# Pairing the key and the query phase chains in the attention stage of a layer kernel on eight cores

## The reference

```python
xn = layernorm(x)
key, value, query = xn @ Wk + bk, xn @ Wv + bv, xn @ Wq + bq
key_phase   = tanh(key @ Wkp + bkp) * phase_scale
query_phase = tanh(query @ Wqp + bqp) * phase_scale
mem_real = cumsum over chunks of 64 tokens of (value * cos(key_phase))
mem_imag = cumsum over chunks of 64 tokens of (value * sin(key_phase))
retrieved = (mem_real * cos(query_phase) + mem_imag * sin(query_phase)) / sqrt(D)
attn = xn + (layernorm(retrieved) * ln_g + ln_b) @ Wo + bo
h = concat([xn, -xn]); w(k) = where(k, 1, -1)
ffn = s2 * (2*relu(s1 * (2*relu(s0 * (h @ w(k0))) @ w(k1))) @ w(k2))
return x + attn + ffn
```

## Time and profile before

| | us |
|---|---|
| median of 3 runs | 2515.23 |
| lowest, highest of them | 2512.86, 2683.95 |
| the profiled execution | 2516.47 |
| its span, from the first to the last instruction of the slowest core (core 5) | 2514.9 |
| spans of the eight cores | 2495.7 to 2514.9 |
| TensorE busy | 1976.2 (79% of the span) |
| VectorE busy | 440.0 (17%) |
| ScalarE busy | 390.3 (16%) |
| GpSimd busy | 89.8 (4%) |

### The profile page before, as it was taken

One profiled execution on the slowest core, in us unless ns is written; L12 is line 12 of the kernel. 1 busy time (PEld: TensorE's weight loads), 2 busy tenths in 40 slices (PEclk: granted clock), 3 DMA queues, 4 the chain that ended last, 5 costly groups with the idle time before them and its releaser, 6 DMA issues.

```text
span 2514.9 us, 21260 instructions; the slowest of 8 cores (2495.7 to 2514.9 us)
## 1 busy us (share of the span) xinstructions
PE 1976.2 (79%) x8836; PEld 868.4 (35%) x8836; DVE 440.0 (17%) x518; ACT 390.3 (16%) x439; POOL 89.8 (4%) x40
## 2 busy tenths in 40 slices
PE   4525435665647769999969999996999996999997
PEld 1213111221224434444424444442344442444443
DVE  0043665555544420000000000000000000000000
ACT  1220333444420002000002000002100001200000
POOL 0001441000000000000000000000000000000000
PEclk9755767777767779999989999998999998999998
DMA  6701569999012346554434645235654343644542
GB/s 102 181 21 35 156 166 168 178 215 186 1 34 96 102 137 170 149 149 135 119 101 135 181 134 146 81 108 176 174 151 136 101 134 117 178 140 136 149 115 69
DMA packets 227081, 324.47 MB, mean 129 GB/s; under 512 B 4645, under 2 KB 103077, under 8 KB 226986
## 3 DMA queue, kind: packets, MB, share of 16 engines
q1 hardware_dynamic: 181930, 235.02, 33.2%
q0 software_dynamic: 32576, 71.31, 16.1%
q10 hardware_dynamic: 12480, 16.78, 1.8%
HBM read 281.16 MB, written 67.11 MB: 138 GB/s over the span
## 4 chain that ended last, share of the span: by engine, by line
PE 73%; DVE 10%; DMA 6%; issue 5%; ACT 5%; DVEq 0%; POOL 0%; ACTq 0%; SPq 0%; POOLq 0%
PE ps L762 36%; PE ps L743 9%; PE ps L790 9%; PE ps L497 4%; PE ps L666 3%; PE ps L352 2%; DMA kst<-k0dbf 2%; DVE wA L519 2%; DVE ph L516 2%; PE ps L714 1%; PE ps L769 1%; PE ps L443 1%; DMA stK<-wkT 1%; PE ps L772 1%; DVE ph L513 1%
## 5 line engine op out<-in xcount | busy, mean ns | idle before, releaser
L762 PE MATMUL ps<-h_sb,kst 128*128 128x512 bf16 x4096 | 901.9, 381 | 10.8 <-DVE rows_sb L725 5.5
L762 PEld LDWEIGHTS ps<-h_sb,kst 128*128 128x128 bf16 x4096 | 397.2, 98 | 511.4 <-issue 47.1
L743 PE MATMUL ps<-xn_sb,kst 128*128 128x512 bf16 x1024 | 230.2, 389 | 84.0 <-DMA kst<-k0dbf 84.0
L719 DVE COPY rowsf_sb<-ps 1x512 f32<-1x512 f32 x8 | 5.4, 678 | 1325.5 <-PE ps L714 1325.5
L790 PE MATMUL ps<-h_sb,kst 128*128 128x512 bf16 x1024 | 223.7, 379 | 6.5 <-DVE rowsf_sb L723 2.2
L776 ACT ACTIVATE h_sb<-ps,cols_sb 128x1024 bf16<-128x1024 f32 x64 | 71.3, 1114 | 932.7 <-PE ps L772 932.7
L534 PE MATMUL ps<-brb,u_sb 128*128 128x512 bf16 x32 | 16.6, 518 | 219.4 <-DVE brb L567 189.8
L743 PEld LDWEIGHTS ps<-xn_sb,kst 128*128 128x128 bf16 x1024 | 101.9, 100 | 212.0 <-issue 97.1
L790 PEld LDWEIGHTS ps<-h_sb,kst 128*128 128x128 bf16 x1024 | 99.0, 98 | 130.5 <-issue 13.5
L748 ACT ACTIVATE h_sb<-ps,cols_sb 128x1024 bf16<-128x1024 f32 x64 | 71.3, 1114 | 415.4 <-PE ps L743 415.4
L666 PE MATMUL ps<-xh_fm,wo_sb 128*128 128x256 bf16 x512 | 84.4, 321 | 29.0 <-DVE x L688 27.5
(11 more groups left out here) (122 smaller groups left out, 1127.3 us busy)
## 6 DMA issues: line engine op xcount, KB each, us to landing
k1bf<-k1t POOLq DMA_DIRECT2D x2, 16384.0 KB, 97.6
kst<-k0dbf SPq DMA_DIRECT2D x64, 512.0 KB, 4.1
xtm_sb<-x_tm SPq DMA_DIRECT2D x16, 512.0 KB, 13.2
st_a<-k0t POOLq DMA_DIRECT2D x8, 1024.0 KB, 8.4
st_b<-k0b POOLq DMA_DIRECT2D x8, 1024.0 KB, 10.2
k0dbf<-st_dd SPq DMA_DIRECT2D x8, 1024.0 KB, 6.8
k2bf<-k2t POOLq DMA_DIRECT2D x1, 8192.0 KB, 116.0
x<-x_fm SPq DMA_DIRECT2D x8, 1024.0 KB, 5.4
```

The source lines that it names most:

```text
L743: e.matmul(ps[:, nco * TF:(nco + 1) * TF], lhsT=kb[:, kc * 256 + nco * 128:kc * 256 + nco * 128 + 128], rhs=xn_v[:, kc, t0:t0 + TF], start ...
L762: e.matmul(ps[:, nco * TF:(nco + 1) * TF], lhsT=kb[:, kc * 256 + nco * 128:kc * 256 + nco * 128 + 128], rhs=h1[:, kc * TF:(kc + 1) * TF], ...
```

## The change

The two calls of `trig_ops` of a group are made one behind the other at the loop's start, and their instructions are emitted in pairs: the key's tanh, the query's tanh, the key's product, the query's product, and so on. The query's chain therefore stands ahead of `bib`, `brb`, the first cumulative sums and the two projections, instead of behind them. Nothing else is changed: the same instructions on the same buffers.

```diff
     a1_A(0)
     for gg in range(NG):
-        a1_emit(trig_ops(PS[1], 0))
+        kp_ops = trig_ops(PS[1], 0)
+        qp_ops = trig_ops(PS[2], 1)
+        for i in range(len(kp_ops)):
+            a1_emit([kp_ops[i], qp_ops[i]])
         P.emit("dve", lambda e: e.tensor_tensor(bib[:], PS[0][:], wA_[0][:], op=ALU.mult),
                reads=[PS[0], wA_[0]], writes=[bib])
...
             tmproj_xn("v", "bv", gg + 1, PS[0])
             tmproj_xn("k", "bkp", gg + 1, PS[1])
-        a1_emit(trig_ops(PS[2], 1))
         a1_combine(gg, 0)
```

## The result

The changed kernel takes 2558.30 us (median of 10 runs) against 2516.29 us (10 runs): 42 us more, a ratio of 1.0166 with a 95% interval of 1.0155 to 1.0177. The forecast was 2546 us, 30 us more, in a range of 2526 to 2570. The sign, the class (slower, but by less than 2%) and the range held; the size came out 12 us short.

A forecast was written before the change was run, and what follows sets the result against it. Bound by the key's ScalarE-VectorE chain, then TensorE's projections, in each gap between attention groups; 5.1 - 5.6 + 38.2 - 8.0 = +29.7 us on 2516.47 gives 2546 us, range 2526 to 2570.

The forecast's parts named there:

- The late gaps: Eleven later gaps between attention groups: each uncovered part grows by 3.47 us, projections' part unchanged; +38.2 us.
- The last group: Final attention group, with no projections following: combine of half 0 starts right behind the sums; -8.0 us.
- The first group: Start of attention: query tanh waits for its projection, first sums at 266.57 instead of 261.46; +5.1 us.
- this subtraction is past: GpSimd's subtraction at 263.63, in the first group: taken as over for the hits, which were counted from 266.6 on.
- The early gaps: First four gaps between groups: 143.3 instead of 148.84 us, three of seven subtractions holding VectorE on the path; -5.6 us.
- the price of a held pair: VectorE instructions held by a GpSimd subtraction in the early gaps: 6.7 us for each of three hits.
- the next falls beside the projections: Early gaps: if one subtraction meets the trigonometric part, the following one comes where blocked VectorE has over 8 us to spare.
- Nothing for the later stages: Stages after attention: they keep their order and shift as a whole, 0 us.
- the subtractions leave the path: Rival, early gaps: GpSimd's subtractions no longer hold the bounding path; 20 us less, 2526 us; chance 0.10.
- all seven stay on it: Rival, early gaps: all seven subtractions hit the bounding path; 27 us on top, 2573 us; chance 0.10.
- TensorE's clock: Rivals, projections after each pause: full clock, 2514 us, chance 0.02; wholly at 1.2 GHz, 2620 us, chance 0.01.
- The rule of the shared port pair: VectorE with two SBUF inputs or in two-port mode and GpSimd exclude each other; products with one PSUM input never held.

The follow-up runs named there:

- The unpaired order: Changed kernel with the query's whole chain behind the key's whole chain, both ahead of bib and brb: 2636.2 us, ratio 1.0480 to the kernel before.
- the four added absolute values: Kernel before with four more absolute values (L515 repeated) in the query's chain of each group: 2564.5 us, ratio 1.0203.
- the key's tail first: Changed kernel with the key's L519, L520, bib and brb ahead of the query's L519 and L520 on VectorE: 2526.4 us, ratio 1.0060 to before.

## Why the prediction was right and where it fell short

**The late gaps: right in mechanism and size.** The walk through the earlier trace rows with two chains gave 3.47 us per gap; measured are 3.48. The unpaired order confirms the same paces (8.7 forecast for it, 8.72 measured), and the four added absolute values confirm that TensorE covered the query's chain before, with little over 1.2 us to spare. The projections' part did not change.

**The last group: right**, 8.0 us earlier.

**The first group: a term mis-sized, +5.1 forecast and +13.1 measured.** By the prediction's own walk the query's L520 starts at 263.46, 0.17 us ahead of the subtraction at 263.63, and no hit was counted. The subtraction came at 261.13 and held the second L519 for 7.7 us. The change did not bring it forward. Counted from the key's first tanh, it starts after 14.53 us on core 5 of the kernel before, but after 12.4 to 13.2 us on its other seven cores, and after 12.4 to 13.3 us on all eight cores of the changed kernel. Core 5 was the exception: GpSimd's idle time ahead of that subtraction was 11.29 us there, and 9.6 to 10.3 on the other seven. Core 1 of the kernel before, 13.22 us after its key's tanh:

```profile
243.74 1.02 ACT L512 ACTIVATE ph<-ps 128x1024 f32<-128x1024 f32 x1
...
256.96 8.07 POOL L465 TENSOR_TENSOR st_dd<-st_a,st_b 128x4096 bf16<-128x4096 bf16 x1 [9.71 <-DMA st_b<-k0b]
```

So the step that failed is the premise that this subtraction is past, taken from the one core on which it came late; the first sums came 25.2 to 25.5 us after the key's tanh on all eight cores of the changed kernel. Without the subtractions they came after 17.47 us, the 5.1 us of the walk.

**The early gaps: right in number, wrong in price (-5.6 forecast, +0.9 measured).** As forecast, three subtractions held VectorE's trigonometric part, but not the three that were named: those that start at 300.66, 340.33 and 380.68 instead of those near 284, 324 and 363. That the count held is in part luck. In three gaps out of four the uncovered part was 28.16, 29.39 and 28.26 us instead of 19.34, which is 8.8 to 10.1 us a gap, not 6.7. Two steps of the prediction failed here.

The first is the price of a held pair. The second L519 (in the third gap the first L520) is due 0.2 to 0.8 us after the subtraction begins, and waits out almost the whole of it: the pair takes 10.07 us instead of 2.36 (9.00 instead of 1.29), 7.7 more, and the first group with and without the subtraction (25.50 and 17.47 us) shows 8.0 in all. The prediction took 6.7, a little over the two waits of the earlier trace rows (6.5 and 5.6) and the mean of 5.7 over seven old hits. Both rows are hits beside the projections, of instructions due 1.3 and 2.2 us into the subtraction, and the mean mixes two prices: the three hits in the uncovered part made it 21.43, 23.92 and 23.60 us instead of 15.86, 5.6 to 8.1 more, and the four beside the projections made that part 4 to 5 us longer, as some of their wait was covered.

The second is L552. The prediction counted the one of half 0 as covered and left out that of half 1, which stands in the uncovered part. It took 1.75, 2.97 and 2.14 us in the three gaps where 0.69 is usual, 1.1 to 2.3 more. Two of them stand here, with the held pair of the first gap between them; the first is held to the end of the subtraction that began at 280.97.

```profile
280.97 7.92 POOL L465 TENSOR_TENSOR st_dd<-st_a,st_b 128x4096 bf16<-128x4096 bf16 x1 [9.62 <-DMA st_b<-k0b]
...
287.70 1.75 DVE L552 SCALAR_TENSOR_TENSOR ret_sb<-ph,cb 128x512 bf16<-128x512 f32 x1
...
299.76 10.07 DVE L519 SCALAR_TENSOR_TENSOR wA<-wA,wB 128x1024 bf16<-128x1024 bf16 x2 [2.20 <-ACT ph L518]
300.66 8.09 POOL L465 TENSOR_TENSOR st_dd<-st_a,st_b 128x4096 bf16<-128x4096 bf16 x1 [9.70 <-DMA st_b<-k0b]
...
326.32 2.97 DVE L552 SCALAR_TENSOR_TENSOR ret_sb<-ph,cb 128x512 bf16<-128x512 f32 x1
```

So "the next falls beside the projections" was true of its start, not of its end.

**Nothing for the later stages: off by 3.4 us the other way.** The product with Wo, 2.3 us of it, ran with TensorE's granted clock a little higher. In its first tile the clock rises 6.0 us after the first matmul before, and 3.8 us after it in the changed kernel (at 750.1 and 791.3 us). A shift of where the clock rises is the likely cause, but no run isolated it. The other 1.1 us are the wait for `kst`, which differs by as much between the cores of one kernel.

**How near the total came is in part luck.** The first group and the early gaps together came out 14.5 us above the forecast, and the late gaps and the product with Wo 3.8 us below it.

**The rivals.** That the subtractions leave the path was wrong. That all seven stay on it was nearer than its 2573 us says: from the one at 261.13 on, all seven reached the path, but three of them only with their last 1.1 to 2.3 us. TensorE's clock was wrong in either direction: the pause grew to 14.54 us, and the projections behind it still took 11.4 us, as after 11.06. This bears out the row on which the prediction relied (0.39 us again within 3.9 us of a pause of 14.56), and of the Trainium skill's warning (TensorE: Matmul & The Clock Gate, "Why this matters for your kernels") it shows that a price once paid in each round is not paid twice. The rule of the shared port pair (SBUF — State Buffer, "Who interferes with whom") agrees with the runs: with the subtractions gone, the means of L516 and L519 are those of an instruction that nothing holds, and with them L552, of two inputs in SBUF, was held as well. The products with one input in PSUM were not: on the eight cores of the changed kernel, none of the L543 and L547 that ran during a subtraction took over 0.69 us.

## What to carry to other kernels

Before an edit moves a chain on an in-order queue, ask what covers it today. Here the query's chain looked like half of the work of two busy engines and cost nothing, as TensorE had 11.4 us of projections beside it; ahead of them it cost 8.7 us a group, and pairing two chains could give only 5.2 back. The same pairing, one group apart and with two of TensorE's projections beneath both chains, made this kernel 3.5% faster. When a walk through a trace passes another engine's work by a fraction of a microsecond, read the same two rows on the other cores before you call it a miss: here seven of eight would have shown the hit. And price a wait by where it falls: a hit beside covered work costs less than one on the path, so a mean over both is too low for the path.

## What the runs showed of the hardware

- A VectorE instruction that is due 0.2 to 0.8 us after a subtraction of GpSimd begins waits for nearly all of its 8 us: 7.7 us for an L519 of 1.2 us or an L520 of 0.69, and 8.0 us for the chain behind it (25.50 us with the subtraction, 17.47 without).
- A gap of about 40 us with two subtractions 20 us apart lost 8.8 to 10.1 us to both: the pair to one, and 1.1 to 2.3 us of L552 to the tail of the other.
- The time of the projections after a pause is not quite steady: 11.4 to 11.6 us in the late groups of the changed kernel, and 10.5 to 11.7, in turn, with the key's tail first, which has the same instructions on TensorE and a pause of 12.99 instead of 14.54 us. Over eleven gaps it makes some 3 us.
